# Graph and mixture-of-experts kernel: four tiles of the first expert issued between the last four transposing turns, three more tiles in other PSUM banks

## What is computed

```
xn       = layernorm(x)
gate     = softmax(xn @ W_gate + b_gate)
adapted  = gate - 0.25 * sigmoid(xn @ W_thr + b_thr)
weights  = adapted where adapted >= 0, divided by their sum over the experts
x        = x + sum over e of weights[:, e] * (xn @ W_exp[e] + b_exp[e])
```

## Time and profile before

| | |
|---|---|
| median of 3 executions | 393.59 us (392.02 to 393.86) |
| profiled execution, time | 392.6 us |
| its span in the trace | 390.8 us |
| TensorE busy | 369.8 us (95%) |
| VectorE busy | 286.8 us (73%) |
| ScalarE busy | 105.3 us (27%) |
| mean granted TensorE clock | 0.991 |

### The profile page before, as it was taken

One profiled execution on the slowest core, in us unless ns is written; L12 is line 12 of the kernel. 1 busy time (PEld: TensorE's weight loads), 2 busy tenths in 40 slices (PEclk: granted clock), 3 DMA queues, 4 the chain that ended last, 5 costly groups with the idle time before them and its releaser, 6 DMA issues.

```text
span 390.8 us, 5935 instructions
## 1 busy us (share of the span) xinstructions
PE 369.8 (95%) x1892; PEld 240.8 (62%) x1892; DVE 286.8 (73%) x440; ACT 105.3 (27%) x189; POOL 6.1 (2%) x33
## 2 busy tenths in 40 slices
PE   0999999999999999979999999999999999999996
PEld 0777787656556563566566666666666666666663
DVE  3799987999988949872895756756767558566653
ACT  4734355556666204554001010010010100100000
POOL 6000000000000000000000000000000000000000
PEclk9999999999999999987999999999999999999999
DMA  8970011222222206300030020300301200000223
GB/s 175 243 239 17 15 39 37 78 67 80 74 73 83 83 14 160 132 28 2 1 107 2 10 99 0 108 0 0 107 0 23 84 0 0 0 0 0 68 91 105
DMA packets 16808, 23.87 MB, mean 61 GB/s; under 512 B 2796, under 2 KB 9683, under 8 KB 16660
## 3 DMA queue, kind: packets, MB, share of 16 engines
q1 hardware_dynamic: 16382, 23.05, 20.0%
q10 hardware_dynamic: 403, 0.53, 0.6%
HBM read 14.77 MB, written 2.56 MB: 44 GB/s over the span
## 4 chain that ended last, share of the span: by engine, by line
PE 80%; DVE 11%; issue 3%; DVEq 2%; DMA 1%; ACT 1%; ACTq 0%
PE ps_g L974 18%; PE ps_g L975 17%; PE ps_g L976 17%; PE ps_g L862 9%; PE ps_w L900 8%; DVE split L632 3%; PE ps_g L848 2%; PE ps_g L938 2%; DVE x_sb L684 2%; DVE stats L597 2%; DMA dst_i<-in_dst_dram 1%; PE ps_w L892 1%; PE ps_a L948 1%; DVEq L648 1%; PE ps_g L850 1%
## 5 line engine op out<-in xcount | busy, mean ns | idle before, releaser
L974 PE MATMUL ps_g<-we_hi,split 128*125 128x512 f16 x320 | 122.3, 382 | 0.4 <-DVE x_sb L758 0.4
L975 PE MATMUL ps_g<-we_lo,split 128*125 128x512 f16 x320 | 122.0, 381 | 0.0
L976 PE MATMUL ps_g<-we_hi,split 128*125 128x512 f16 x320 | 122.0, 381 | 0.0
L758 DVE SCALAR_TENSOR_TENSOR x_sb<-ps_g,weight_s,x_sb 125x512 f32<-125x512 f32 x80 | 59.9, 749 | 56.2 <-PE ps_g L976 56.1
L632 DVE TENSOR_TENSOR split<-places,keys 125x1536 f16<-125x1536 int16 (+2 forms) x125 | 91.3, 794 | 7.8 <-PE ps_w L900 4.2
L763 DVE SCALAR_TENSOR_TENSOR x_sb<-late,weight,x_sb 125x512 f32<-125x512 f32 x80 | 59.9, 750 | 9.5 <-DVE x_sb L758 5.5
L974 PEld LDWEIGHTS ps_g<-we_hi,split 128*125 128x125 f16 x320 | 44.1, 138 | 26.2 <-DVE x_sb L758 0.8
L976 PEld LDWEIGHTS ps_g<-we_hi,split 128*125 128x125 f16 x320 | 44.0, 137 | 25.8 <-issue 0.6
L975 PEld LDWEIGHTS ps_g<-we_lo,split 128*125 128x125 f16 x320 | 44.0, 138 | 25.4 <-issue 0.6
L900 PE MATMUL ps_w<-split 125*128 125x250 f16 x402 | 53.7, 270 | 3.4 <-DVE split L632 1.8
L900 PEld LDWEIGHTS ps_w<-split 125*128 125x128 f16 x402 | 36.8, 97 | 22.4 <-issue 9.7
(11 more groups left out here) (129 smaller groups left out, 193.0 us busy)
## 6 DMA issues: line engine op xcount, KB each, us to landing
stage<-in_L_ffn_W_exp_dram SPq DMA_DIRECT2D x8, 1024.0 KB, 5.3
late<-counts SPq DMA_DIRECT2D x50, 122.1 KB
x_sb<-in_x_dram SPq DMA_DIRECT2D x5, 448.0 KB, 11.2
out_dram<-x_sb SPq DMA_DIRECT2D x10, 224.0 KB
late<-in_L_ffn_b_exp_dram SPq DMA_DIRECT2D x1, 2000.0 KB
w_sb<-in_L_gnn_W_dram SPq DMA_DIRECT2D x2, 512.0 KB, 11.6
x_sb<-in_x_dram ACTq DMA_DIRECT2D x1, 260.0 KB
out_dram<-x_sb ACTq DMA_DIRECT2D x10, 26.0 KB
```

Source lines behind the costliest of these rows:

```text
L758: nc.vector.scalar_tensor_tensor(out=x_sb[:, i, :], in0=ps_exp[(TILES * par + i) % RING], scalar=weight_s[:, ds(e, 1), i], in1=x_sb[:, i, ...
L974: nc.tensor.matmul(bank, xhi[:, k, tokens[i]], hi_w, start=(k == 0), stop=False)
L975: nc.tensor.matmul(bank, xhi[:, k, tokens[i]], lo_w, start=False, stop=False)
L976: mm = nc.tensor.matmul(bank, xlo[:, k, tokens[i]], hi_w, start=False, stop=(k == KD - 1))
```

## The change

Seven banks serve the ten tiles of expert 0. Tiles 0 to 3 use the four `ps_exp` banks, tile 4 `ps_w[0]`, tile 5 `ps_a`, tile 6 `ps_w[1]`, tiles 7 and 8 `ps_exp[0]` and `ps_exp[1]` again, tile 9 `ps_w[0]` again. VectorE reads each tile where it lies. Tile 0 is issued behind turn 6 and `gate(5)`, tile 1 behind turn 7 and `gate(6)`, tile 2 behind turn 8 and `gate(7)`, tile 3 behind turn 9 and `gate(8)`; then `gate(9)` and tiles 4 to 9. The waits of these ten tiles follow from the banks: the `y` tile read for 0 to 4, the `xlo` of tile 8 made for tile 5 and that of tile 9 for tile 6, and for tiles 7, 8 and 9 the adds of tiles 0, 1 and 4. The waits of the other experts and their banks are as before.

```
+        ps_first = ps_exp + [ps_w[0][0:R, :], ps_a[0:R, :], ps_w[1][0:R, :]]
+        FIRST_AT = (0, 1, 2, 3, 4, 5, 6, 0, 1, 4)
+        FILL_AT = TILES - RING
@@ add_expert
-                nc.vector.scalar_tensor_tensor(out=x_sb[:, i, :], in0=ps_exp[(TILES * par + i) % RING],
+                first = isinstance(e, int) and e == 0
+                nc.vector.scalar_tensor_tensor(out=x_sb[:, i, :], in0=ps_first[FIRST_AT[i]] if first else ps_exp[(TILES * par + i) % RING],
@@ expert_tile
-                if isinstance(e, int) and TILES * e + i < RING:
-                    pe.wait_ge(x1_ready, min(YS + 2 + i, TILES))
+                if not isinstance(e, int) or e > 0:
+                    pe.wait_ge(acc_step, TILES * e + i + 1)
+                    bank = ps_exp[(TILES * par + i) % RING]
                 else:
-                    pe.wait_ge(acc_step, TILES * e + i + 1)
-                bank = ps_exp[(TILES * par + i) % RING]
+                    bank = ps_first[FIRST_AT[i]]
+                    if FIRST_AT[i] in FIRST_AT[:i]:
+                        pe.wait_ge(acc_step, RING + 1 + FIRST_AT.index(FIRST_AT[i]))
+                    elif i < RING:
+                        pe.wait_ge(x1_ready, YS + 2 + i)
+                    elif i == RING:
+                        pe.wait_ge(x1_ready, YS + 1)
+                    else:
+                        pe.wait_ge(xlo_ready, TILES - 2 + i - RING)
@@ first_pass of TensorE
-                    if i == TILES - 2:
+                    if i == FILL_AT:
                         pe.wait_ge(we_lo_done, 1)
-                        expert_tile(0, 0, 0)
-                expert_tile(0, 0, 1)
+                    if i >= FILL_AT:
+                        expert_tile(0, 0, i - FILL_AT)
                 gate(TILES - 1)
-                for i in range(2, TILES):
+                for i in range(RING, TILES):
                     expert_tile(0, 0, i)
```

## The result

| | before | after |
|---|---|---|
| median of 6 executions of each | 391.97 us | 388.26 us (387.03 to 388.8) |
| profiled execution, its span | 390.8 us | 386.4 us |
| mean granted clock of TensorE | 0.991 | 0.995 |

The ratio is 0.9888, with a 95% interval of 0.9855 to 0.9920: 4.4 us less, between 3.1 and 5.7. The two medians of the table lie 3.7 us apart, inside that interval. The forecast was 388.3 us, from a gain of 4.7.

A forecast was written before the change was run, and what follows sets the result against it. TensorE bounds the kernel, losing time in the join before expert 0. Expert 0 ends 5.88 us earlier, a new 1.16 us stall leaves 4.72 us gain, from 393.0 to 388.3 us; range 386.6 to 390.4 us.

The forecast's parts named there:

- The fill: Join before expert 0: tiles 0 to 3 behind turns 6 to 9; four tiles done, not two, at `gate(9)`, 183.82 us.
- The two waits and the low clock: TensorE before turns 7 and 8: waits of 1.11 and 1.33 us plus 2.9 us of slow clock, 5.3 us in all.
- The seven banks: Expert 0's tiles 4 to 9 run without waiting for adds; expert 0 ends at 199.82 us, 5.88 us earlier.
- The adds and the new stall: VectorE's adds go only 0.1 us earlier; expert 1's first tile waits 1.16 us for the seventh, starting at 200.98.
- the unchanged count: Wait of expert 1's tile 0, left as before, which holds it until the seventh add ends at 200.92 us.
- The sum: Expert 1's start moves from 205.70 to 200.98 us: gain 4.72 us, forecast 388.3 us, chance 0.81.
- The clock did not fall in the new stall: Rival: clock falls in the 1.16 us stall before expert 1, costing up to 3.4 us: 391.7 us, chance 0.09.
- The turns kept their slack: Rival in the fill: turns 8 and 9 wait 1 us each for ScalarE, despite 1.3 us slack: 390.3 us, chance 0.05.
- The fill did not lose the clock: Rival: clock falls at 173 us and stays low until `gate(9)`, 6.1 us lost: 399.1 us, chance 0.03.
- the slower side: Outcome that the changed kernel measures slower, by the clock lost in the fill: chance 0.03.

The follow-up runs named there:

- the spare matmuls: Kernel before plus unread 512-column matmuls, four ahead of turn 7 and five ahead of turn 8: ratio 0.9934, expert 1 33.06 us after turn 6.
- five banks: Changed kernel with five banks in place of seven for expert 0's tiles: ratio 0.9953 to the kernel before, expert 1 33.54 us after turn 6.
- the second set of executions: The changed kernel run once more, unedited, as measure for the two kernels that alter the weights' work: ratio 0.989 to the kernel before, median 387.32 us.

## Why the prediction was right

*The fill.* Reckoned from turn 6: tile 0 at 0.89 us, turns 7, 8 and 9 at 3.51, 6.99 and 10.47, `gate(9)` at 13.95. Measured: 0.90, 3.52, 7.01, 10.49 and 13.97. Turn-to-tile pieces read at full clock in the trace before could be laid end to end because nothing but TensorE's own queue bound them. The two waits and the low clock were given back in full, and the spare matmuls confirm the clock's part: 2.8 us, where 2.9 was reckoned.

*The seven banks.* Expert 0 ends at 197.51 + 2.59 = 200.10, 29.97 us after turn 6; reckoned 29.95. With five banks, and with the old ring, TensorE stalls at the very adds that the same working gives.

*The adds and the new stall.* The first add was reckoned 19.33 us after turn 6 and came at 19.35. The stall was reckoned at 1.16 us and is 201.26 - 200.10 = 1.16. That the 2.28 us of weights ahead of the sixth add set its length is shown by taking them away (stall gone) and by doubling them (2.33 us more). The prediction named "the unchanged count" as what makes TensorE wait, but did not see that the bank itself was free by then.

*The sum.* 4.72 us forecast, 4.70 by the trace. That the median of 388.26 agrees with 388.3 is partly luck, as two misses of 1.0 us cancel: the level of the kernel before was taken at 393.0 from four executions and measures 391.97, and the medians lie 3.7 us apart and not 4.7. In the second set of executions the change has 387.32 us against 391.5. Both ratios, 0.9888 and 0.989, say 4.3 to 4.4 us, and 4.7 lies within their intervals.

*The rivals.* The clock did not fall in the new stall, in either profile of the change, and none of its twelve executions has a mean clock below 0.995, where the kernel before has 0.991 with its fall in the join. The section of the Trainium skill that spoke for it ("TensorE: Matmul & The Clock Gate", "A second HAM failure mode: psum-queue depth-cycling") is not borne out by one or two waits of this length: waits for an add of 0.38, 0.99 and even 2.97 us between long matmuls left the clock at 1.00. With 3.33 us, in the kernel that makes the weights twice, the clock did fall, and it cost 2.8 us in the profile, of the up to 3.4 allowed for. The turns kept their slack: turn 8's `xn` was there at 175.57, 1.6 us before the turn. The fill did not lose the clock. What the prediction did not see is that the slower side had another way in: with the old ring of four the same order makes a stall of 5.62 us that takes the clock down, and the change would have been a loss.

## What to carry to other kernels

Filling an idle engine with work from further on gains only if that work's results have somewhere to lie until their reader starts: count the buffers up to the reader's first release, or the idle time comes back in one piece, behind the filled stretch. When an order is to be changed, find the chain that the change does not move (here the adds, from the last gate on) and price the new end against it. Look at what that chain carries that is not urgent: 2.28 us of weight splitting in idle time upstream removed the last stall. And when tiles move to other banks, work out every later wait on those banks anew: here the count of expert 1 still spoke of a bank that had long been free.

## What the runs showed of the hardware

In the join the granted clock fell to the 1.2 GHz level in three cases: in the second of two gaps of 0.97 and 1.19 us with a turn and a gate of short matmuls between them, in a gap of 3.33 us, and in one of 5.62 us. It held at 2.4 GHz through 0.97 or 1.19 us alone beside the same short matmuls, and through 0.99 us and 2.97 us between long ones. By the traces the falls cost 2.8, 2.8 and 2.4 us, in this order. These are single profiles (two for 0.99 us and for the pair of gaps), and they don't make a rule by the gap's length: executions of one kernel differ. Of 65 executions of the kernel before, beside the experiments, 58 have a mean clock of 0.983 to 0.991, six have 0.995, and one has 0.999 and took 388.75 us, so there the two gaps cannot have cost the 6.8 us at the low level that they cost in the profile.

There is another fall that comes in some executions only. It begins between 143.3 and 144.7 us, behind the one-column matmuls that sum the degrees (from 140.7 to about 143 us in the first profile of the change), in code that is the same in all kernels here; 5 of 12 profiles show it and 7 don't. The change had it in its first profile and not in its second, in this order:

```profile
140.00:145.00 5.00, 5.00 (x29) 3.83 (x28) 1.98 (x4) 0.00 (x0) 0.00 (x0) 0.88 0.00 0
145.00:150.00 5.00, 4.42 (x8) 1.30 (x7) 5.00 (x9) 2.38 (x3) 0.00 (x0) 0.78 0.23 45
```

```profile
140.00:145.00 5.00, 5.00 (x30) 3.89 (x29) 2.21 (x5) 0.00 (x0) 0.00 (x0) 1.00 0.00 0
145.00:150.00 5.00, 4.42 (x10) 1.52 (x9) 5.00 (x8) 2.38 (x3) 0.00 (x0) 1.00 0.54 152
```

Turn 6 starts at 170.13 us in the one and at 169.16 in the other, and their spans differ by 1.0 us, as much as a small change is worth. Not all of that need be the clock: in the seven profiles without this fall turn 6 starts anywhere from 168.79 to 169.87 us. That is why the joins above are measured from turn 6. What decides in which execution it falls stays open.
